# Second layer: value products of three of twelve key tiles as three rounded passes, scores three key tiles ahead, four buffers of probabilities

## The chip, the cores and the metric

The kernel runs on one core of one Trainium2 chip. A core has a matrix engine (PE, with its weight loads listed apart as PEld), a vector engine (DVE), a scalar engine (ACT), a general engine (POOL) and a queue engine for transfers (SP). They run side by side and order themselves by counting semaphores. The metric is the device time of one execution in microseconds (us), median of the runs. Lower is better.

## The reference, cut to what matters

Two layers of cross-attention and feed-forward over 16 batches of 56 tokens of width 256; the keys and values of both attentions come from the same context of 1500 rows of width 128 per batch. The change touches the attention of the second layer only:

```python
q = rmsnorm((hidden_states @ Wq).reshape(B, Sq, H, D), gq)      # 16 batches, 56 tokens, 16 heads, 128
k = rmsnorm((encoder_hidden_states @ Wk).reshape(B, Skv, H, D), gk)   # 1500 keys
v = (encoder_hidden_states @ Wv).reshape(B, Skv, H, D)
scores = jnp.einsum('bqhd,bkhd->bhqk', q, k) * scale
attn = jax.nn.softmax(scores, axis=-1)
out = jnp.einsum('bhqk,bkhd->bqhd', attn, v)
```

## The kernel before, in words

The kernel does not form k and v. The queries of a batch are folded through Wk beforehand, so that a score is a product of the folded query (128 x 896: 16 heads by 56 tokens, held in two halves of 448 columns) with the raw context, times one factor per key and head (`m.rk`). In the same way the probabilities multiply the raw context (`nat`, rows of keys), and Wv and Wo are applied once, after the loop.

`second_attention` goes through 16 batches, each of 12 key tiles of 125 keys. For one key tile:

- PE, `scores_half` (L1058 to L1060): each half of the scores is three passes of rounded 32-bit operands (type fp32r): query high by context low, query low by context high, high by high. "High" is the rounded value and "low" the rest, both made beforehand: `high_parts` on ACT (L906, L907), `low_parts` on POOL (L961), `query_low` on DVE (L998). The result lies in one of two pairs of PSUM banks (`slots`, t % 2).
- DVE, `scale_scores` (L993): multiplies by `m.rk` into one of two `scaled` buffers.
- ACT, `exp` (L918): writes the probabilities into one of NP = 3 buffers `P`.
- POOL, `add` (L968 for the first two tiles together, then L971): sums the probabilities into `acc`.
- PE, `values_half` (L1074): one full fp32 product per half, which shows as two records of PE, summed over the 12 tiles in `psO`.

Scores run LAG = 2 tiles ahead of the values: at step t, PE makes the scores of tile t+2 (from step 10 on those of the next batch), then the values of tile t. Scores of tile t+2 wait until tile t is scaled. At step 0 of a batch, PE also makes `sums` of the batch before (L1086: ones by `acc`), between scores and values.

The order of DVE is written out in its `body`. In step t it scales tile t+LAG. At step 0 it then takes the reciprocal of the sums of the batch before (`invert`, two instructions, L1006); at step 1, after the scaling, it multiplies the result of the batch before by it (`normalise`, two instructions, L1014, all operands in SBUF); at step 6 it runs `query_low` (at step 7 in batch 0). ACT copies the values out of PSUM at the end of a batch (`values_out`, L924) and makes the high parts for the batch after next at step NT - LAG. POOL makes the low part of the next context after the last add of a batch, then waits for `sums` before its first add (L968). Each engine takes its instructions in the order of the program.

Ahead of the loop, PE makes eight products of weights (`fold`), five before and three after the first scores; ACT and DVE copy them out (`keep_fold`).

Of the kernel before, what the change touches and what calls it, by code (L numbers as in the profile page):

```python
# [8 lines left out]
F32 = mybir.dt.float32  # L9
F32R = mybir.dt.float32r  # L10
BF16 = mybir.dt.bfloat16
U8 = mybir.dt.uint8
ALU = mybir.AluOpType
ACT = mybir.ActivationFunctionType
# [3 lines left out]
S, C = 1500, 128  # L18
H, HD, G0 = 16, 128, 8
KT, NT = 125, 12  # L20
QW, HALF = H * QS, H * QS // 2
# [70 lines left out]
def need(eng, sem, value):  # L92

    if isinstance(value, int) and value <= 0:
        return
    eng.wait_ge(sem, value)
# [27 lines left out]
def semaphores(sem, tag, names):  # L124

    return namedtuple("Semaphores", names)(*[sem(f"{tag}_{n}") for n in names])
# [290 lines left out]
def batches(eng, body):  # L417

    for b in range(B):
        body(b, b % 2, b + 1 < B, b + 2 < B)  # L420
# [9 lines left out]
def first_attention(nc, m, a, tag, sem):  # L430
# [6 lines left out]
    with ExitStack() as ctx:  # L437
# [8 lines left out]
        qlo = [m.qlo0, sb("qlo1", [C, QW], F32R)]  # L446
        P = [sb(f"probs{i}", [KT, QW], F32) for i in range(NP)]
        acc = sb("acc", [KT, QW], F32)
# [404 lines left out]
def second_attention(nc, m, a, tag, sem):  # L853

    s = semaphores(sem, tag, [
        "ld_land", "ld_nat0", "ld_nat1", "ctx_hi", "ctx_lo", "q_hi", "q_lo", "scores", "scaled", "probs", "pv", "acc",
        "den", "inv", "o_raw", "o_done", "fold_pe", "fold_act", "fold_dve", "y_pe", "y_act"])
    LAG, NP = 2, 3
    with ExitStack() as ctx:
        sb = lambda n, sh, dt: ctx.enter_context(nc.sbuf_tensor(f"{tag}_{n}", sh, dt))  # L860
        psum = lambda n, sh: ctx.enter_context(nc.psum_tensor(f"{tag}_{n}", sh, F32))
# [3 lines left out]
        nat = [m.nat0, sb("nat1", [KT, NT, C], F32)]  # L865
        qhi = [sb(f"qhi{i}", [C, QW], F32R) for i in range(2)]
        qlo = [sb(f"qlo{i}", [C, QW], F32R) for i in range(2)]
        scaled = [sb(f"scaled{i}", [KT, QW], F32) for i in range(2)]
        P = [sb(f"probs{i}", [KT, QW], F32) for i in range(NP)]
        acc = sb("acc", [KT, QW], F32)  # L870
        inv = sb("inv", [C, 2, HALF], F32)
        norm_banks = psum("norm", [128, 2, 512])
        slots = psum("slots", [128, 2, 2, 512])
        psO = psum("psO", [128, 2, 512])
# [25 lines left out]
        @block.scalar  # L900
        def _(act):
            def high_parts(b, par):

                need(act, s.ld_land, 16 * b)
                need(act, s.scores, NT * (b - 1))
                act.activation(chi[par][:, :], land[:, :], ACT.Copy).then_inc(s.ctx_hi, 1)  # L906
                act.activation(qhi[par][:, :], m.qs[:, bass.ds(b, 1), :, :].rearrange("p o h q -> p (o h q)"),  # L907
                               ACT.Copy).then_inc(s.q_hi, 1)

            def exp(b, par, t):  # L910

                need(act, s.pv, NT * b + t + 1 - NP)
                if t >= NP:
                    need(act, s.acc, (NT - 1) * b + max(1, t - NP))
                else:
                    need(act, s.acc, (NT - 1) * b + t + 1 - NP)
                act.wait_ge(s.scaled, NT * b + t + 1)
                act.activation(P[t % NP][:, :], scaled[t % 2][:, :], ACT.Exp).then_inc(s.probs, 1)  # L918

            def values_out(b):  # L920

                act.wait_ge(s.pv, NT * b + NT)
                dst = m.qs[:, bass.ds(b, 1), :, :].rearrange("p o (a h) q -> p (o a) (h q)", a=2)
                act.activation(dst, psO[:, :, 0:HALF], ACT.Copy).then_inc(s.o_raw, 1)  # L924

            def body(b, par, nxt, nxt2):
                for t in range(NT):
                    if b == 0 and t == 3:
                        high_parts(1, 1)
                    if t == NT - LAG and nxt2:  # L930
                        high_parts(b + 2, par)
                    for bt, tt in tile_ahead(LAG, b, t):
                        exp(bt, bt % 2, tt)
                values_out(b)

            def keep_fold(i):

                act.wait_ge(s.fold_pe, i + 1)
                act.activation(fold_rows(i), fold_bank(i), ACT.Copy).then_inc(s.fold_act, 1)

            first = S // 4
            act.activation(chi[0][:, 0:first], land[:, 0:first], ACT.Copy).then_inc(s.ctx_hi, 1)
            act.activation(qhi[0][:, :], m.qs[:, 0, :, :].rearrange("p h q -> p (h q)"), ACT.Copy).then_inc(s.q_hi, 1)
            act.activation(chi[0][:, first:S], land[:, first:S], ACT.Copy).then_inc(s.ctx_hi, 1)
            for i in (0, 2, 4):
                keep_fold(i)
            exp(0, 0, 0)
            keep_fold(6)
            exp(0, 0, 1)
            batches(act, body)  # L950
            act.wait_ge(s.ctx_lo, B + 1)
            for i in range(KC):
                act.wait_ge(s.y_pe, i + 1)
                act.activation(land[:, HALF * i:HALF * i + HALF], slots[:, 0, i, 0:HALF], ACT.Copy).then_inc(s.y_act, 1)
# [30 lines left out]
        @block.vector  # L985
        def _(dve):
            def scale_scores(b, par, t):

                dve.wait_ge(s.scores, NT * b + t + 1)
                need(dve, s.probs, NT * b + t - 1)  # L990
                src = slots[0:KT, t % 2, :, 0:HALF].rearrange("p a (h q) -> p a h q", q=QS)
                rk = m.rk[:, bass.ds(b, 1), t, :].rearrange("p o (a h) -> p (o a) h", a=2).unsqueeze(3)
                dve.tensor_tensor(scaled[t % 2][:, :].rearrange("p (a h q) -> p a h q", a=2, q=QS), src,  # L993
                                  rk.to_broadcast([KT, 2, H // 2, QS]), ALU.mult).then_inc(s.scaled, 1)

            def query_low(b, par):
                dve.wait_ge(s.q_hi, b + 1)
                dve.tensor_tensor(qlo[par][:, :], m.qs[:, bass.ds(b, 1), :, :].rearrange("p o h q -> p (o h q)"),  # L998
                                  qhi[par][:, :].bitcast(F32), ALU.subtract).then_inc(s.q_lo, 1)

            def invert(b):

                dve.wait_ge(s.den, b + 1)
                need(dve, s.o_done, 2 * b)
                for half in range(2):
                    dve.reciprocal(inv[:, half, :], norm_banks[:, half, 0:HALF]).then_inc(s.inv, 1)  # L1006

            def normalise(b):

                dve.wait_ge(s.o_raw, b + 1)  # L1010
                o = m.qs[:, bass.ds(b, 1), :, :].rearrange("p o (a h) q -> p (o a) (h q)", a=2)
                for half in range(2):
                    dve.wait_ge(s.inv, 2 * b + half + 1)
                    dve.tensor_tensor(o[:, half, :], inv[:, half, :], o[:, half, :], ALU.mult).then_inc(s.o_done, 1)  # L1014

            def body(b, par, nxt, nxt2):
                start = isinstance(b, int) and b == 0
                for t in range(NT):
                    for bt, tt in tile_ahead(LAG, b, t):
                        scale_scores(bt, bt % 2, tt)  # L1020
                    if t == 0 and not start:
                        invert(b - 1)
                    if t == 1 and not start:
                        normalise(b - 1)
                    if nxt and t == (7 if b == 0 else 6):
                        query_low(b + 1, 1 - par)

            def keep_fold(i):

                dve.wait_ge(s.fold_pe, i + 1)  # L1030
                dve.tensor_copy(fold_rows(i), fold_bank(i)).then_inc(s.fold_dve, 1)

            query_low(0, 0)
            for i in (1, 3):
                keep_fold(i)
            for t in range(LAG):
                scale_scores(0, 0, t)
            for i in (5, 7):
                keep_fold(i)
            batches(dve, body)  # L1040
            invert(B - 1)
            normalise(B - 1)

        @block.tensor
        def _(pe):
# [18 lines left out]
            def values_half(b, par, t, half):  # L1064
                if half == 0:
                    pe.wait_ge(s.probs, NT * b + t + 1)
                    if t == 0:
                        need(pe, (s.ld_nat0, s.ld_nat1)[par], 8 * (b + par))
                        need(pe, s.o_raw, b)
                        if b == 0:  # L1070
                            pe.wait_ge(s.fold_act, 2)
                            pe.wait_ge(s.fold_dve, 2)
                cols = slice(HALF * half, HALF * half + HALF)
                last = pe.matmul(psO[:, half, 0:HALF], nat[par][:, t, :], P[t % NP][:, cols], start=t == 0, stop=t == NT - 1)  # L1074
                if half == 1:
                    last.then_inc(s.pv, 1)

# [885 lines left out]
```

## Time and profile before

| What | Value |
|---|---|
| Median of 3 runs | 2141.82 us (2140.28 to 2142.17) |
| The profiled execution | 2140.49 us |
| Its span | 2138.7 us |
| PE busy in the span | 2089.7 us (98%) |
| DVE busy | 1638.7 us (77%) |
| ACT busy | 1082.3 us (51%) |
| POOL busy | 1417.7 us (66%) |

The loop of the second attention lies between about 1370 and 1930 us of the span. A row of a timeline gives start, duration, engine, line, operation, output and inputs with their shapes, how many instructions were merged into it (x4), and in brackets how long the engine had been idle before it and who released it. Matmul records overlap, since an end includes the way through the array; the distance between starts tells what a pass costs. Rows of a line give minimum, median and maximum duration in ns.

### The profile page before, as it was taken

How to read it: one execution, taken by the hardware profiler on the slowest of the kernel's cores; microseconds unless marked ns; L12 is line 12 of the kernel's file. 1: busy time of each engine (PE TensorE's matmuls, PEld its weight loads, DVE VectorE, ACT ScalarE, POOL GpSimd, SP SyncE). 2: the span in 40 equal slices, each digit the busy share in tenths (PEclk: the TensorE clock that was granted, in tenths of full speed). 3: DMA queues.
4: the chain of work that ended last, by engine and by line, in shares of the span. 5: the costliest groups of instructions: out<-in, count | busy, mean ns of one | idle time of the engine just before them, and what ended most of it. 6: DMA issues, size and time to landing. Idle time of an engine off the chain costs nothing. (4 is left out here: it accounts for less than half of the span.)

```text
span 2138.7 us, 27497 instructions
## 1 busy us (share of the span) xinstructions
PE 2089.7 (98%) x8514; PEld 1520.4 (71%) x8514; DVE 1638.7 (77%) x2584; ACT 1082.3 (51%) x3401; POOL 1417.7 (66%) x1062
## 2 busy tenths in 40 slices
PE   7999999999999999999999899999999999999999
PEld 7777677777777777777777468666666666665998
DVE  4889999999999999999997765556666665642577
ACT  3565555655665556555556328543434444332433
POOL 1477787778777878788777336287877878761221
PEclk9999999999999999999999999999999999999999
DMA  3000000000000000000001310011111111101110
GB/s 134 30 15 16 29 29 15 24 21 30 16 29 15 30 29 15 15 29 30 15 11 40 135 54 1 30 44 57 45 43 55 33 58 29 44 0 52 38 53 25
DMA packets 15140, 75.64 MB, mean 35 GB/s; under 512 B 1746, under 2 KB 2114, under 8 KB 13986
## 3 DMA queue, kind: packets, MB, share of 16 engines
q1 hardware_dynamic: 14994, 73.89, 10.5%
q8 instruction: 68, 1.11, 0.2%
q14 instruction: 78, 0.64, 0.1%
HBM read 72.97 MB, written 0.92 MB: 35 GB/s over the span
## 5 line engine op out<-in xcount | busy, mean ns | idle before, releaser
L539 ACT ACTIVATE l_prod_act<-l_prod_act 125x128 f32<-125x128 f32 x1152 | 343.8, 301 | 353.0 <-DVE l_prod_act L714 353.0
L634 POOL TENSOR_TENSOR l_prod<-l_prod 125x256 f32<-125x256 f32 x480 | 350.4, 737 | 239.6 <-DVE l_prod L714 239.4
L971 POOL TENSOR_TENSOR l_acc<-l_acc,l_probs 125x896 f32<-125x896 f32 x160 | 346.3, 2164 | 81.4 <-ACT l_probs L918 65.9
L714 DVE TENSOR_TENSOR l_prod<-l_side,xq 125x512 f32<-125x512 f32 x480 | 325.6, 678 | 45.1 <-PE l_side L823 38.7
L993 DVE TENSOR_TENSOR l_scaled<-l_slots,rk 125x896 f32<-125x896 f32 x192 | 207.0, 1084 | 198.8 <-PE l_slots L1060 198.7
L918 ACT ACTIVATE l_probs<-l_scaled 125x896 f32<-125x896 f32 x192 | 183.1, 954 | 318.7 <-DVE l_scaled L993 293.5
L628 POOL TENSOR_TENSOR l_acc<-l_acc,l_probs 125x896 f32<-125x896 f32 x160 | 339.2, 2120 | 0.0
L557 ACT ACTIVATE l_probs<-l_slots,mask_bias 125x448 f32<-125x448 f32 x384 | 225.5, 624 | 59.7 <-PE l_slots L775 54.1
L684 DVE SCALAR_TENSOR_TENSOR top<-l_side,mask_bias,top 125x448 f32<-125x448 f32 x330 | 217.1, 666 | 8.0 <-PE l_side L806 8.0
L539 ACT ACTIVATION_READ_ACCUMULATOR l_prod_act<-l_prod_act 125x1 f32 x1152 | 219.1, 190 | 0.0
L723 DVE TENSOR_REDUCE l_msq<-l_prod 125x4 f32<-125x256 f32 x480 | 197.3, 412 | 22.3 <-POOL l_prod L634 22.3
L714 DVE TENSOR_TENSOR l_prod_act<-l_side,xq 125x512 f32<-125x512 f32 x288 | 197.3, 685 | 16.6 <-PE l_side L823 13.9
L1058 PE MATMUL l_slots<-l_qhi,l_clo 128*125 128x448 f32 x384 | 203.2, 529 | 0.0
L822 PE MATMUL l_side<-norm_lo,l_chi 128*125 128x512 f32 x384 | 198.3, 516 | 0.4 <-DVE l_prod L714 0.2
L822 PE MATMUL l_side<-norm_lo,chi 128*125 128x512 f32 x384 | 196.4, 511 | 0.2
L784 PE MATMUL l_psO<-l_probs,spare 125*128 125x448 f32 x384 | 174.6, 539 | 0.0
L784 PE MATMUL l_psO<-l_probs,l_nat 125*128 125x448 f32 x384 | 174.6, 539 | 0.0
L1074 PE MATMUL l_psO<-l_probs,nat 125*128 125x448 f32 x384 | 160.0, 538 | 0.0
L1074 PE MATMUL l_psO<-l_probs,l_nat 125*128 125x448 f32 x384 | 159.7, 538 | 0.0
L823 PE MATMUL l_side<-norm_hi,chi 128*125 128x512 f32 x384 | 151.5, 394 | 0.0
L823 PE MATMUL l_side<-norm_hi,l_chi 128*125 128x512 f32 x384 | 151.3, 394 | 0.0
L1059 PE MATMUL l_slots<-l_qlo,l_chi 128*125 128x448 f32 x384 | 140.4, 366 | 0.0
(261 smaller groups left out, 4619.4 us busy)
## 6 DMA issues: line engine op xcount, KB each, us to landing
land<-in_ctxT SPq DMA_DIRECT2D x32, 750.0 KB, 4.2
l_nat<-in_ctxN SPq DMA_DIRECT2D x16, 750.0 KB
post_we<-in_experts SPq DMA_DIRECT2D x20, 384.0 KB, 3.0
spare<-in_ctxN SPq DMA_DIRECT2D x8, 750.0 KB
nat<-in_ctxN SPq DMA_DIRECT2D x8, 750.0 KB
spare<-in_wo SPq DMA_DIRECT2D x2, 2048.0 KB, 9.0
spare<-in_wqT SPq DMA_DIRECT2D x4, 512.0 KB, 8.8
mid_fac<-in_factors SPq DMA_DIRECT2D x1, 2048.0 KB, 7.6
```

What stands on the lines that cost most here:

```text
L539: last = act.activation(whole, whole, ACT.Copy, accum_out=msq[:, t, 4 * g + c:4 * g + c + 1])
L557: act.activation(P[t % NP][:, HALF * i:HALF * i + HALF], bank_of("S", t, i)[0:KT, 0:HALF], ACT.Exp, bias=m.mask_bias[:, b, t:t + 1]).then_ ...
L628: pool.tensor_tensor(acc[:, :], acc[:, :], P[t % NP][:, :], ALU.add).then_inc(s.acc, 1)
L634: pool.tensor_tensor(buf[:, :, 0:C // 2], buf[:, :, 0:C // 2], buf[:, :, C // 2:C], ALU.add).then_inc(s.half_sum, 1)
L684: dve.scalar_tensor_tensor(top[:, cols], bank, bias, top[:, cols], ALU.add, ALU.max).then_inc(s.side_dve, 1)
L714: dve.tensor_tensor(to[:, :, :], bank, xt.unsqueeze(1).to_broadcast([KT, 4, C]), ALU.mult).then_inc(s.side_dve, 1)
L784: last = pe.matmul(psO[:, half, 0:HALF], nat[b % 2][:, t, :], P[t % NP][:, cols], start=t == 0, stop=t == NT - 1)
L822: pe.matmul(bank[0:KT, :], chi[b % 2][:, keys], m.norm_lo[:, cols], start=True, stop=False)
L823: last = pe.matmul(bank[0:KT, :], chi[b % 2][:, keys], m.norm_hi[:, cols], start=False, stop=True)
L971: pool.tensor_tensor(acc[:, :], acc[:, :], P[t % NP][:, :], ALU.add).then_inc(s.acc, 1)
L993: dve.tensor_tensor(scaled[t % 2][:, :].rearrange("p (a h q) -> p a h q", a=2, q=QS), src, rk.to_broadcast([KT, 2, H // 2, QS]), ALU.mult) ...
L1074: last = pe.matmul(psO[:, half, 0:HALF], nat[par][:, t, :], P[t % NP][:, cols], start=t == 0, stop=t == NT - 1)
```

## The change

LAG becomes 3 and NP becomes 4. For key tiles 3, 6 and 9 of each batch the fp32 product of a half is replaced by three rounded passes: values low by probabilities high, values high by probabilities low, high by high. The parts of the probabilities are made per tile, high on ACT after the exponential, low on DVE; those of the values once per batch for the three tiles together (125 x 384), for the next batch at step 11.

```diff
-    LAG, NP = 2, 3
+    LAG, NP = 3, 4
+    SPLIT = [3, 6, 9]
+    tiles_split = slice(3, 10, 3)
...
+            def probs_high(b, t):
+                at = SPLIT.index(t)
+                act.wait_ge(s.probs, NT * b + t + 1)
+                act.activation(phi[at % 2][:, :], P[t % NP][:, :], ACT.Copy).then_inc(s.p_hi, 1)
+            def values_high(b):
+                need(act, (s.ld_nat0, s.ld_nat1)[b % 2], 8 * (b + b % 2))
+                need(act, s.pv, NT * (b - 1) + SPLIT[-1] + 1 if b > 0 else 0)
+                act.activation(nat_hi[:, :, :], nat[b % 2][:, tiles_split, :], ACT.Copy).then_inc(s.p_hi, 1)
...
                     for bt, tt in tile_ahead(LAG, b, t):          # ACT
                         exp(bt, bt % 2, tt)
+                        if tt in SPLIT:
+                            probs_high(bt, tt)
+                    if t == SPLIT[-1] + 2 and nxt:
+                        values_high(b + 1)
                 values_out(b)
...
+            values_high(0)
             for i in (0, 2, 4):
                 keep_fold(i)
             exp(0, 0, 0)
             keep_fold(6)
             exp(0, 0, 1)
+            exp(0, 0, 2)
...
+            def probs_low(b, t):
+                at = SPLIT.index(t)
+                dve.wait_ge(s.p_hi, (len(SPLIT) + 1) * b + at + 2)
+                dve.tensor_tensor(plo[at % 2][:, :], P[t % NP][:, :], phi[at % 2][:, :].bitcast(F32), ALU.subtract).then_inc(s.p_lo, 1)
+            def values_low(b):
+                dve.wait_ge(s.p_hi, (len(SPLIT) + 1) * b + 1)
+                dve.tensor_tensor(nat_lo[:, :, :], nat[b % 2][:, tiles_split, :], nat_hi[:, :, :].bitcast(F32),
+                                  ALU.subtract).then_inc(s.p_lo, 1)
...
                     for bt, tt in tile_ahead(LAG, b, t):          # DVE
                         scale_scores(bt, bt % 2, tt)
+                    if t + 2 in SPLIT:
+                        probs_low(b, t + 2)
+                    if t == SPLIT[-1] + 2 and nxt:
+                        values_low(b + 1)
                     if t == 0 and not start:
                         invert(b - 1)
                     if t == 1 and not start:
                         normalise(b - 1)
...
             query_low(0, 0)
+            values_low(0)
...
                 cols = slice(HALF * half, HALF * half + HALF)     # PE
-                last = pe.matmul(psO[:, half, 0:HALF], nat[par][:, t, :], P[t % NP][:, cols], start=t == 0, stop=t == NT - 1)
+                if t in SPLIT:
+                    at = SPLIT.index(t)
+                    pe.wait_ge(s.p_lo, (len(SPLIT) + 1) * b + at + 2)
+                    pe.matmul(psO[:, half, 0:HALF], nat_lo[:, at, :], phi[at % 2][:, cols], start=False, stop=False)
+                    pe.matmul(psO[:, half, 0:HALF], nat_hi[:, at, :], plo[at % 2][:, cols], start=False, stop=False)
+                    last = pe.matmul(psO[:, half, 0:HALF], nat_hi[:, at, :], phi[at % 2][:, cols], start=False, stop=False)
+                else:
+                    last = pe.matmul(psO[:, half, 0:HALF], nat[par][:, t, :], P[t % NP][:, cols], start=t == 0, stop=t == NT - 1)
```

## Rows read from the trace of the kernel before

**Rows 1.** Busy time by engine in 1720 to 1800 us: busy (count), granted clock.
```profile
core 0: us, PE busy (x) PEld busy (x) DVE busy (x) ACT busy (x) POOL busy (x), PEclk, DMA share, GB/s
1720.00:1800.00 80.00, 80.00 (x291) 53.77 (x290) 53.77 (x42) 31.87 (x34) 61.88 (x28) 1.00 0.19 56
```

**Rows 2.** Timeline of PE, one key tile of the second attention.
```profile
1630.23 1.67 PE L1074 MATMUL l_psO<-l_probs,l_nat 125*128 125x448 f32 x4
1631.94 0.36 PE L1059 MATMUL l_slots<-l_qlo,l_chi 128*125 128x448 f32 x1
1632.14 0.36 PE L1060 MATMUL l_slots<-l_qhi,l_chi 128*125 128x448 f32 x1
1632.94 1.67 PE L1074 MATMUL l_psO<-l_probs,l_nat 125*128 125x448 f32 x4
```

**Rows 3.** Timeline of PE, rounded passes with 128 weight columns, last stage.
```profile
2060.16 0.36 PE L1808 MATMUL post_bk<-post_xhi,post_wlo 128*128 128x448 f32 x1
2060.36 0.36 PE L1809 MATMUL post_bk<-post_xlo,post_whi 128*128 128x448 f32 x1
```

**Rows 4.** Timeline of all engines, start of a batch (its values from 1616.48).
```profile
1614.98 1.67 PE L1086 MATMUL l_norm<-l_acc,ones 125*128 125x448 f32 x4
1616.48 1.67 PE L1074 MATMUL l_psO<-l_probs,l_nat 125*128 125x448 f32 x4
1616.68 5.77 DVE L1006 RECIPROCAL l_inv<-l_norm 128x448 f32<-128x448 f32 x2 [0.41 <-PE l_norm L1086]
1616.79 2.10 POOL L968 TENSOR_TENSOR l_acc<-l_probs 125x896 f32<-125x896 f32 x1 [2.09 <-PE l_norm L1086]
1619.04 2.09 POOL L971 TENSOR_TENSOR l_acc<-l_acc,l_probs 125x896 f32<-125x896 f32 x1
1622.37 1.03 DVE L993 TENSOR_TENSOR l_scaled<-l_slots,rk 125x896 f32<-125x896 f32 x1
1623.31 1.15 DVE L1014 TENSOR_TENSOR qs<-l_inv,qs 128x448 f32<-128x448 f32 x2
1623.51 0.95 ACT L918 ACTIVATE l_probs<-l_scaled 125x896 f32<-125x896 f32 x1 [6.17 <-DVE l_scaled L993]
1623.76 0.36 PE L1059 MATMUL l_slots<-l_qlo,l_chi 128*125 128x448 f32 x1
1624.54 14.02 POOL L971 TENSOR_TENSOR l_acc<-l_acc,l_probs 125x896 f32<-125x896 f32 x6 [3.42 <-ACT l_probs L918]
```

**Rows 5.** Instructions by line: ns minimum/median/maximum.
```profile
L998 DVE TENSOR_TENSOR l_qlo<-qs,l_qhi x16: 1144/2425/2452, 1366.5 to 1874.6; 128x896 fp32r<-128x896 f32 x16
L1014 DVE TENSOR_TENSOR qs<-l_inv,qs x32: 560/612/621, 1417.2 to 1931.3; 128x448 f32<-128x448 f32 x32
```

**Rows 6.** Timeline of DVE and POOL around one `query_low`.
```profile
1599.16 5.04 POOL L971 TENSOR_TENSOR l_acc<-l_acc,l_probs 125x896 f32<-125x896 f32 x2
1599.80 2.42 DVE L998 TENSOR_TENSOR l_qlo<-qs,l_qhi 128x896 fp32r<-128x896 f32 x1
```

**Rows 7.** Timeline of DVE and POOL between the layers; last row: L1186 by line.
```profile
1289.54 1.56 DVE L1186 TENSOR_SCALAR mid_xn<-x,mid_meanvar,mid_rstd 112x256 f32<-112x256 f32 x2
1289.73 1.21 POOL L1264 TENSOR_TENSOR mid_sql<-mid_sq,mid_sqh 128x448 fp32r<-128x448 f32 x1 [0.26 <-ACT mid_sqh L1335]
1289.86 1.24 DVE L1186 TENSOR_SCALAR mid_xn<-x,mid_meanvar,mid_rstd 112x256 f32<-112x256 f32 x1
...
L1186 DVE TENSOR_SCALAR mid_xn<-x,mid_meanvar,mid_rstd x16: 400/410/1246, 1245.4 to 1289.9; 112x256 f32<-112x256 f32 x16
```

**Rows 8.** Groups of instructions by line and shape: count, busy us, mean ns.
```profile
L907 ACT ACTIVATE l_qhi<-qs 128x896 fp32r<-128x896 f32 x15 | 14.0, 936 | 0.0
L523 ACT ACTIVATE l_chi<-land 128x375 fp32r<-128x375 f32 x8 | 4.0, 502 | 0.0
L961 POOL TENSOR_TENSOR l_clo<-land,l_chi 128x1500 fp32r<-128x1500 f32 x15 | 51.1, 3409 | 0.0
```

**Rows 9.** The longest waits of PE for a vector result, and the windows around it.
```profile
PE pre_bk L405 <- DVE top L276: 3.4, 1, 3.4
PE mid_bk L1441 <- POOL mid_sql L1264: 2.2, 3, 1.1
...
21.00:24.00 3.00, 2.27 (x12) 0.50 0.32 133
24.00:27.00 3.00, 3.00 (x18) 0.57 0.16 66
```

More of the change, by code:

```diff
@@ L855, in second_attention @@
     s = semaphores(sem, tag, [
-        "ld_land", "ld_nat0", "ld_nat1", "ctx_hi", "ctx_lo", "q_hi", "q_lo", "scores", "scaled", "probs", "pv", "acc",
+        "ld_land", "ld_nat0", "ld_nat1", "ctx_hi", "ctx_lo", "q_hi", "q_lo", "scores", "scaled", "probs", "p_hi", "p_lo", "pv", "acc",
         "den", "inv", "o_raw", "o_done", "fold_pe", "fold_act", "fold_dve", "y_pe", "y_act"])
-    LAG, NP = 2, 3
+    LAG, NP = 3, 4
+    SPLIT = [3, 6, 9]
+    tiles_split = slice(3, 10, 3)
     with ExitStack() as ctx:
@@ L869, in second_attention @@
         P = [sb(f"probs{i}", [KT, QW], F32) for i in range(NP)]
+        phi = [sb(f"phi{i}", [KT, QW], F32R) for i in range(2)]
+        plo = [sb(f"plo{i}", [KT, QW], F32R) for i in range(2)]
+        nat_hi = sb("nat_hi", [KT, len(SPLIT), C], F32R)
+        nat_lo = sb("nat_lo", [KT, len(SPLIT), C], F32R)
         acc = sb("acc", [KT, QW], F32)
```

## The prediction

> **What bounds the kernel now.** I read the busy shares by engine first, then those of the loop that is changed, then its timeline tile by tile. In the loop PE is busy all the time at the full granted clock, while DVE has 67% and POOL 77% [rows 1]: what counts is PE's own work, and any moment at which another engine is late for it. In a tile [rows 2] the four fp32 records begin at 1630.23 and the sixth score pass ends where the next four begin, 1632.94: 2.71 us. The sums, also four fp32 records, take from 1614.98 to 1616.48, 1.50 us [rows 4]; the six score passes have the rest, 0.20 us each (1631.94 to 1632.14). So PE needs 12 x 2.73 + 1.50 = 34.3 us for a batch and idles hardly at all. The one place with little slack is the start of a batch. There two reciprocals hold DVE for 5.77 us, the scaling behind them ends at 1623.40 (1622.37 + 1.03), and the score passes that wait for it are about 0.1 us late: from the value product's start at 1621.94 the second score pass is normally 1.71 us off [as in rows 2] and here begins at 1623.76, 1.82 us off [rows 4].
>
> **Part 1, PE work.** A half of a split tile drops two fp32 records (0.75 us) for three rounded passes. Weights 128 columns wide do not slow such a pass: 0.20 us [rows 3]. With 0.205 a tile goes from 1.50 to 1.23 us, 0.27 less; 3 tiles x 16 batches x 0.27 = 13.0 us off PE. The number of score tiles stays the same.
>
> **Part 2, added side work of a batch.** ACT: three copies of 125x896 at 0.94 and one of 125x384 at about 0.51 us [rows 8], 3.3 us on an engine with 40% in the loop [rows 1]; hidden. DVE: three subtractions of the form of `query_low`, both inputs in SBUF, 1.14 us alone and 2.42 us usually [rows 5], and one of 384 columns, about 0.5 us. That puts DVE at some 30 of 36 us, so its order matters.
>
> **Part 3, what DVE's two-input work costs beside POOL.** `query_low` begins at 1599.80, in the middle of an add that began at 1599.16 and takes 2.10; it ends at 1602.22, that is 0.96 us after that add ended at 1601.26; and the second add, due by then, ends at 1604.20, 1.98 us after the subtraction [rows 6]. They don't share: one waits until the other is through. The Trainium skill says the same (SBUF — State Buffer, "Who interferes with whom"): a DVE instruction with two inputs in SBUF contends with a GpSimd instruction that reads SBUF, and the lock is held for the whole instruction by whichever came first. By that rule, and the trace agrees here, an instruction of DVE pays for the whole add in flight.
>
> **Part 4, the start of a batch.** Zero is the start of the first value product (1616.48 in [rows 4]); handing over costs 0.20 us from PE to DVE, 0.11 from DVE to ACT, 0.08 from ACT to POOL, about 0.16 from DVE to PE, and DVE begins the next instruction some 0.09 before the end of one (all from [rows 4], the last two from 1622.37 + 1.03 = 1623.40 against 1623.76 - 0.20 and 1623.31).
> - DVE: with LAG 3, scaling of tile 3 comes before the reciprocals and is off their way; they still begin at 0.20; the scaling of tile 4 takes 5.89 to 6.92, the place that tile 3 had.
> - PE: values 0 to 1.50, scores 4 to 2.73, values 1 to 4.23, scores 5 to 5.47, values 2 to 6.97; scores 6 wait for scaled tile 4 until 7.08, as late as today, and end at 8.31.
> - POOL: adds begin at 0.31, 2.56 and 4.80 (2.10 each); the third ends at 6.90. The fourth waits for exp of tile 4 (7.03 to 7.98) and is due at 8.06.
> - DVE: low part of tile 3 from 6.83, POOL quiet from 6.90: 1.14 us, ends at 8.0. Values 3 on PE are due at 8.31 and end at 9.54: in time.
> - Then `normalise`, before the scaling of tile 5. Today it meets no add: POOL is idle until 1624.54 [rows 4], and the 32 instructions take 560 to 621 ns [rows 5]. Now the first half runs from 7.91 to 8.52, and the fourth add comes in at 8.06 and stands first in line when the half is done. It ends at 8.52 + 1.98 = 10.50, and only then comes the second half: 10.50 + 0.48 = 10.98. Scaling of tile 5 ends near 11.95, and scores 7, which need it, start at 12.1 instead of 9.54.
>
> That is a stall of 2.55 us in each of the 15 batches that have one before them: 38 us. Bounds for this wait, of which the trace has no case: below, both halves pass before the add, 0.6 us (9.04 for `normalise`, 10.0 for the scaling, 10.15 for PE); above, both halves wait for an add each, 2 x 2.1 more than alone, but the fifth add itself needs tile 5, so the second add can't be there, which leaves about 2.8. I take 2.55, since in [rows 7] an instruction of POOL that comes in during the third of four DVE instructions (1289.73, between 1289.54 and 1289.94) gets ahead of the fourth, which takes 1.24 instead of 0.41 us.
>
> What follows in the batch has slack. Behind the stall, the low part of tile 6 waits at most one add (about 2.3 us) and is done at 16.4 while values 6 are due at 18.9; `query_low`, scaling of tile 10 and the low part of tile 9 end at 24.9 for values 9 at 26.8. At the end POOL's low part of the context (3.41 us [rows 8]) ends at about 35.0; `values_low` is due at 34.9, ends at 35.45, and scaling of tile 3 at 36.4, when the reciprocals begin anyway (36.3 + 0.2). Each 0.1 us by which POOL is later there costs 15 x 0.1. A batch thus takes 34.3 + 0.1 - 0.8 + 2.55 = 36.2 us.
>
> **Part 5, outside the steady loop.** Before the first batch, the third score tile waits for the first to be scaled, and the last `fold` for a copy that DVE makes after scaling tile 2: I reckon the first values about 2.0 us later, of which 1.23 is a score tile made ahead: 0.8 us lost. Batch 0 has no `normalise`.
>
> **Sum.** -13.0 + 38.3 + 0.8 = +26 us. On the profiled execution (2140.5) that is 2166.6; the median of the runs is 1.3 above it: 2168.
>
> **Rivals.**
> - *Both halves before the add* (the other side). If DVE keeps its port between two instructions that overlap by 0.09 us, `normalise` is through at 9.04. The stall is then 0.6 us: -13.0 + 15 x 0.6 + 0.8 = -3.2, 2139. It decides at a stall of 0.8 us (12.2/15). For it: the second half is issued at 8.43, before the first has ended. Against: [rows 7]. 17%.
> - *Sharing.* If both engines just slow down, `normalise` runs 2.1 times as long behind 8.06 (2.42 against 1.14 in [rows 5]) and ends at 10.2, 0.8 earlier than forecast: stall 1.8, +15, 2157. [Rows 6] speak against it. With it go cases in which only part of the batches meet the add. 14%.
> - *POOL late at the end.* If its low part of the context slips by 0.5 us, `values_low` and all behind it slip too: another 7 us, 2175. Part of the forecast's own range. 6%.
> - *The clock falls.* After PE had waited 3.4 us for DVE near the start, the granted clock went to 0.50, the 1.2 GHz level, for the windows from 21 us on; after waits of 1.1 us at most it did not [rows 9]. 2.55 us lies between. Some 6 us at half the clock would cost 3 us a batch: +45 more, 2213. 5%.
> - *The split saves nothing*, because weights of 125 rows or fp32r operands written by ACT and DVE make the passes dearer: it would need 0.25 us a pass, seen nowhere. 2%.
>
> **How the numbers follow.** The forecast itself has 56%, with 2162 to 2176 as its own range (stall of 2.3 to 2.8, POOL's slip). Adding sharing and the first rival takes the range from 2137 to 2177, which leaves out the clock and tails. A change under 0.2%, 4.3 us, can't be told from none in such a measurement. The first rival is 3 us faster, so it counts mostly as no change (0.11) and partly as faster (0.08); the rest, 0.81, is slower.
>
> **What would show it.** The value rows of tiles 3, 6, 9 as six passes 0.20 us apart. Pairs of `normalise` of some 3.1 us from start to end in place of 1.15, with an add between. PE idle before the scores of tile 7, released by the scaling, 2.5 us x 15; values never waiting for a low part. A batch from reciprocal to reciprocal of 36.2 us against 34.3. I am wrong if `normalise` stays at 1.2 us, if the stall is at another tile, or if the clock leaves 1.00 in the loop.

## The result, and the profile after

The changed kernel takes 2186.1 us (median of 4 runs, 2185.2 to 2187.0) against 2142.0 before: ratio 1.0207, 95% interval 1.0189 to 1.0225. It is 44 us slower; forecast were 26 us, 2168, with a range that ended at 2177.

The loop was to be read first, and within it one batch against another. The first fence has the windows of two neighbouring batches of the changed kernel, from the start of the values of one to that of the next, and below them that of an earlier batch.

```profile
core 0: us, PE busy (x) PEld busy (x) DVE busy (x) ACT busy (x) POOL busy (x), PEclk, DMA share, GB/s
1638.59:1672.73 34.14, 33.80 (x132) 24.18 (x130) 25.04 (x22) 17.48 (x19) 28.96 (x12) 1.00 0.14 42
1672.73:1710.37 37.64, 35.38 (x132) 25.33 (x131) 29.25 (x22) 17.57 (x19) 28.73 (x12) 0.95 0.15 45
1413.73:1449.97 36.24, 33.96 (x132) 24.18 (x130) 27.22 (x22) 17.47 (x19) 28.71 (x12) 1.00 0.15 44
```

All do the same work. The second takes 3.5 us longer, PE is idle for 2.3 us of it, and the granted clock averages 0.95 in place of 1.00. Of the 15 batches that have one before them, 13 are like it. One more, from 1413.73, has the wait but keeps the clock. Only the one from 1638.59 has neither. The timeline of the second, with the rows that answer to [rows 4]:

```profile
1672.73 1.67 PE L1122 MATMUL l_psO<-l_probs,nat 125*128 125x448 f32 x4
1672.93 5.77 DVE L1042 RECIPROCAL l_inv<-l_norm 128x448 f32<-128x448 f32 x2
1678.62 1.03 DVE L1017 TENSOR_TENSOR l_scaled<-l_slots,rk 125x896 f32<-125x896 f32 x1
1679.56 1.08 DVE L1029 TENSOR_TENSOR l_plo<-l_probs,l_phi 125x896 fp32r<-125x896 f32 x1
1680.56 3.07 DVE L1050 TENSOR_TENSOR qs<-l_inv,qs 128x448 f32<-128x448 f32 x2
1680.79 2.35 POOL L995 TENSOR_TENSOR l_acc<-l_acc,l_probs 125x896 f32<-125x896 f32 x1 [1.19 <-ACT l_probs L924]
1681.04 0.37 PE L1118 MATMUL l_psO<-l_phi,l_nat_lo 125*128 125x448 f32 x1
1682.05 0.37 PE L1120 MATMUL l_psO<-l_phi,l_nat_hi 125*128 125x448 f32 x1
1683.55 2.08 DVE L1017 TENSOR_TENSOR l_scaled<-l_slots,rk 125x896 f32<-125x896 f32 x2
1684.68 0.73 PE L1099 MATMUL l_slots<-l_qhi,l_clo 128*125 128x448 f32 x1 [2.27 <-DVE l_scaled L1017]
1685.22 0.57 PE L1100 MATMUL l_slots<-l_qlo,l_chi 128*125 128x448 f32 x1
1685.59 0.57 PE L1101 MATMUL l_slots<-l_qhi,l_chi 128*125 128x448 f32 x1
```

The pair of multiplications takes 3.07 us where it took 1.15 [rows 4], with an add between its halves: its second half, seen by itself, runs from 1681.10 to 1683.63, and the add ends at 1683.14. Behind it the scaling of tile 5 begins at 1683.55, and PE, through with the values of tile 3 at 1682.25, starts the scores of tile 7 only at 1684.68. From then on the passes are 0.37 us apart instead of 0.20: the clock has fallen. The window over that stretch, columns as above but PE alone:

```profile
1684.70:1688.10 3.40, 3.40 (x8) 0.51 0.00 0
```

In the batch from 1638.59 the exponential of tile 4 came 0.28 us later, for a reason that the trace doesn't show, and with it the add. Its record now begins as good as together with that of the second multiplication (1646.93 and 1646.95), where it was 0.3 us ahead of it in the other batch (1680.79 and 1681.10):

```profile
1645.42 1.08 DVE L1029 TENSOR_TENSOR l_plo<-l_probs,l_phi 125x896 fp32r<-125x896 f32 x1
1646.42 1.16 DVE L1050 TENSOR_TENSOR qs<-l_inv,qs 128x448 f32<-128x448 f32 x2
1646.93 2.61 POOL L995 TENSOR_TENSOR l_acc<-l_acc,l_probs 125x896 f32<-125x896 f32 x1 [1.46 <-ACT l_probs L924]
1646.95 0.62 DVE L1050 TENSOR_TENSOR qs<-l_inv,qs 128x448 f32<-128x448 f32 x1
1648.62 0.47 PE L1099 MATMUL l_slots<-l_qhi,l_clo 128*125 128x448 f32 x1 [0.34 <-DVE l_scaled L1017]
```

(The last DVE row is the second half alone, which the row before the add counts too.) Here the pair took 1.16 us, the add had to wait instead (2.61 us), PE was 0.5 us late and the clock stayed up.

### The profile page after: what moved, and what is told of

The parts are those of the page before. It is cut to its first block and busy times, and to the rows that moved or that the text cites. A ratio compares the mean times of both kernels' runs of the same rounds, so it can differ in the third digit from the quotient of the medians.

```text
span 2185.2 us, 27879 instructions
## 1 busy us (share of the span) xinstructions
PE 2103.0 (96%) x8610; PEld 1553.4 (71%) x8610; DVE 1751.1 (80%) x2648; ACT 1130.8 (52%) x3465; POOL 1443.1 (66%) x1062
## 5 line engine op out<-in xcount | busy, mean ns | idle before, releaser
L995 POOL TENSOR_TENSOR l_acc<-l_acc,l_probs 125x896 f32<-125x896 f32 x160 | 371.8, 2324 | 76.1 <-ACT l_probs L924 63.4
L628 POOL TENSOR_TENSOR l_acc<-l_acc,l_probs 125x896 f32<-125x896 f32 x160 | 339.1, 2120 | 0.0
L1099 PE MATMUL l_slots<-l_qhi,l_clo 128*125 128x448 f32 x384 | 193.0, 503 | 34.2 <-DVE l_scaled L1017 32.7
L784 PE MATMUL l_psO<-l_probs,l_nat 125*128 125x448 f32 x384 | 174.6, 539 | 0.0
L1101 PE MATMUL l_slots<-l_qhi,l_chi 128*125 128x448 f32 x384 | 145.7, 380 | 0.0
L1100 PE MATMUL l_slots<-l_qlo,l_chi 128*125 128x448 f32 x384 | 145.5, 379 | 0.0
L1099 PEld LDWEIGHTS l_slots<-l_qhi,l_clo 128*125 128x125 f32 x384 | 74.0, 193 | 77.8 <-DVE l_scaled L1017 49.0
```

Source lines behind the costliest of these rows:

```text
L628: pool.tensor_tensor(acc[:, :], acc[:, :], P[t % NP][:, :], ALU.add).then_inc(s.acc, 1)
L784: last = pe.matmul(psO[:, half, 0:HALF], nat[b % 2][:, t, :], P[t % NP][:, cols], start=t == 0, stop=t == NT - 1)
L995: pool.tensor_tensor(acc[:, :], acc[:, :], P[t % NP][:, :], ALU.add).then_inc(s.acc, 1)
L1099: pe.matmul(out, clo[par][:, keys], qhi[par][:, cols], start=True, stop=False)
```

## The experiments

The theory after the result had two links: (1) an add of POOL gets in between the two multiplications of DVE and holds the second back, because both have two inputs in SBUF; (2) the wait of PE that this makes is just long enough to bring the clock down, which costs 1.5 us more. The rivals: the longer lead, or the load on DVE as such, or dear split passes; and for the clock, that it only shows the idle time.

**The lead and the buffers alone** (`SPLIT = []`, the parts of the values left out).

> The score lead of three tiles and the four buffers alone, no split tile. Theory (port order, then clock): the two multiplications follow the scaling of tile 4 at once, from 6.83 to 7.95 after the start of a batch's values, before the add that is due at 8.06; no collision, the clock stays at 1.00. Only the start-up cost of about 1 us is left: 2143 us, within 0.2% of before. Rival (the longer lead itself is the cost, by the order of DVE or by more buffers in flight): 10 us or more above before, with PE stalled once per batch.

2142.8 us, ratio 1.0007 (0.9997 to 1.0016). The pair and the add, from its timeline:

```profile
1660.28 1.15 DVE L1045 TENSOR_TENSOR qs<-l_inv,qs 128x448 f32<-128x448 f32 x2
1661.51 4.34 POOL L990 TENSOR_TENSOR l_acc<-l_acc,l_probs 125x896 f32<-125x896 f32 x2 [1.19 <-ACT l_probs L922]
```

The pair is through 0.08 us before the add. The lead costs about 1 us by itself, which can't be told from nothing.

**The inverse kept in PSUM.** The sums, which overwrite it there, now wait for the multiplications.

```diff
-                    dve.reciprocal(inv[:, half, :], norm_banks[:, half, 0:HALF]).then_inc(s.inv, 1)
+                    dve.reciprocal(norm_banks[:, half, 0:HALF], norm_banks[:, half, 0:HALF]).then_inc(s.inv, 1)
...
-                    dve.tensor_tensor(o[:, half, :], inv[:, half, :], o[:, half, :], ALU.mult).then_inc(s.o_done, 1)
+                    dve.tensor_tensor(o[:, half, :], norm_banks[:, half, 0:HALF], o[:, half, :], ALU.mult).then_inc(s.o_done, 1)
...
-                need(pe, s.inv, 2 * b)
+                need(pe, s.o_done, 2 * b)
```

> The changed kernel, but the reciprocals are written back into PSUM, so that each of the two multiplications has only one input in SBUF; order and amount of work are the same. Theory: they take 0.6 to 0.7 us each beside the adds, 1.2 to 1.4 us a pair instead of 3.07; the wait before the scores of tile 7 falls from 2.45 to 0.6 to 0.9 us, and the clock stays at 1.00: -13.3 + 15 x 0.75 + 2.5 = about 0, 2142 us (2138 to 2146). Rival (DVE is simply overloaded by the low parts, or the split passes are dear): stays above 2170.

2141.5 us, ratio 0.9999 (0.9990 to 1.0009): 44 us are back by the place of one operand.

```profile
1661.10 1.15 DVE L1049 TENSOR_TENSOR qs<-l_norm,qs 128x448 f32<-128x448 f32 x2
1661.34 2.11 POOL L994 TENSOR_TENSOR l_acc<-l_acc,l_probs 125x896 f32<-125x896 f32 x1 [1.23 <-ACT l_probs L923]
1663.30 0.47 PE L1098 MATMUL l_slots<-l_qhi,l_clo 128*125 128x448 f32 x1 [0.34 <-DVE l_scaled L1016]
```

The add begins 0.24 us behind the pair and runs beside it; neither is longer for it. The order, the low parts and the split passes are those of the changed kernel, so none of these costs the 44 us by itself.

**One multiplication instead of two**, the inverse in SBUF as in the changed kernel (counts of `o_done` halved).

```diff
-                for half in range(2):
-                    dve.wait_ge(s.inv, 2 * b + half + 1)
-                    dve.tensor_tensor(o[:, half, :], inv[:, half, :], o[:, half, :], ALU.mult).then_inc(s.o_done, 1)
+                dve.wait_ge(s.inv, 2 * b + 2)
+                dve.tensor_tensor(o, inv[:, :, :], o, ALU.mult).then_inc(s.o_done, 1)
```

> The changed kernel with the two multiplications of 448 columns written as one of 896, at the same place, all inputs in SBUF. Theory (an add gets in only between two instructions of DVE, never inside one): it starts at 7.83, before the add that is due at 8.06, takes 1.1 us, and the add waits instead; the wait before the scores of tile 7 is 0.5 to 0.6 us, the clock stays at 1.00: 2142 us (2139 to 2144), as with the reciprocals in PSUM. Rival (two-input work beside adds is slow by sharing): the pair still takes 2.4 us or more, 2160 or above.

2142.3 us, ratio 1.0003 (0.9994 to 1.0012).

```profile
1661.32 1.08 DVE L1049 TENSOR_TENSOR qs<-l_inv,qs 128x896 f32<-128x896 f32 x1
1661.56 2.82 POOL L995 TENSOR_TENSOR l_acc<-l_acc,l_probs 125x896 f32<-125x896 f32 x1 [1.19 <-ACT l_probs L924]
```

The same operands, the same place, the same collision: whole, the multiplication isn't touched, and the add pays (2.82 against 2.10 us in [rows 4]). That rules out sharing, under which both would be slow, and shows the gap between two instructions as the place of the loss.

**PE kept busy while it waits** (8, then 4 passes, whose results nothing uses).

```diff
                 for t in range(NT):
+                    if t == 4 and not start:
+                        pe.wait_ge(s.inv, 2 * b)
+                        for i in range(8):
+                            pe.matmul(norm_banks[0:KT, i % 2, 0:HALF], chi[par][:, 0:KT], qhi[par][:, 0:HALF], start=True, stop=True)
```

> The changed kernel with eight more rounded passes (1.64 us) on PE, put between the values of tile 3 and the scores of tile 7, where PE waits; their result is used nowhere. They shorten the idle time from 2.45 to about 0.8 us and leave the wait's end where it is. Theory (the fall of the clock is a cost of its own, 1.5 us in 13 batches): clock 1.00 all through, 2186 - 20 = 2166 us, although more is computed. Rival (the granted clock only echoes the idle time, the whole loss is the wait): 2186 us or more.

2169.3 us, ratio 1.0130 (1.0115 to 1.0145): 17 us less than the changed kernel, with 120 matmuls more.

> As filler8, with four unused passes (0.82 us) in place of eight: PE is idle for 1.6 us before the scores of tile 7. Which idle time brings the clock down is open between 1.1 us (it held, in the kernel before) and 2.27 us (it fell). If 1.6 us is short enough the clock stays at 1.00 and the time is that of filler8, 2169 us; if not, 2186 us as for the changed kernel.

2169.5 us, ratio 1.0131 (1.0117 to 1.0145). With four passes PE is idle for 1.46 us; its timeline, then the window around it:

```profile
1674.33 0.97 PE L1144 MATMUL l_norm<-l_qhi,l_chi 128*125 128x448 f32 x4
1676.77 0.47 PE L1099 MATMUL l_slots<-l_qhi,l_clo 128*125 128x448 f32 x1 [1.46 <-DVE l_scaled L1017]
```

```profile
1674.00:1678.00 4.00, 2.54 (x13) 1.00 0.00 0
```

So the clock is a cost of its own, beside the wait that stays.

**The two multiplications one step later**, in both forms (`if t == 2 and not start: normalise(b - 1)`). With the inverse in SBUF:

> The changed kernel with the two multiplications one step later, behind the scaling of tile 5, and both inputs still in SBUF: the position alone, without the change of place of the reciprocals. Theory (the port goes to whoever asked first, for a whole instruction): the first multiplication is due at 8.9 while the fourth add runs till 10.16, the fifth add is due before it ends and gets in ahead of the second; the pair ends at 13.1, scaling of tile 6 at 14.1, and PE waits 1.9 us before the scores of tile 8 in place of tile 7: 2132 + 15 x 1.9 = 2160 us if the clock holds, up to 2180 if it falls. Rival (only the place at step 1 is bad, one step of slack is enough): 2132 us as with the reciprocals in PSUM.

2169.0 us, ratio 1.0130 (1.0116 to 1.0144).

```profile
1676.28 4.28 DVE L1050 TENSOR_TENSOR qs<-l_inv,qs 128x448 f32<-128x448 f32 x2
1680.48 2.08 DVE L1017 TENSOR_TENSOR l_scaled<-l_slots,rk 125x896 f32<-125x896 f32 x2
1681.61 0.47 PE L1099 MATMUL l_slots<-l_qhi,l_clo 128*125 128x448 f32 x1 [1.73 <-DVE l_scaled L1017]
```

The pair now meets two adds, 4.28 us, and PE waits a tile later: its scores start 14.16 us after the values; the scaling before them was expected to end at 14.1. The time is 9 us above the 2160 that I gave for it; a batch takes 35.9 in place of 35.5 us, and I haven't followed the rest. With the inverse in PSUM:

> As the one with the reciprocals in PSUM, and the two multiplications come one step later, behind the scaling of tile 5. Theory: scaling of tile 5 ends at about 9.0 and that of tile 6 at 11.2, before PE needs them at 9.5 and 12.3: no wait in the batch is left, the gain of the split shows: 2142 - 13.3 + 2.5 = 2131 us (2129 to 2134). Rival (the split saves less than 0.27 us a tile in place): 2138 or more.

2131.9 us, ratio 0.9957 (0.9942 to 0.9972): faster than both kernels, by 10 and by 54 us. One of its batches:

```profile
1649.56:1683.16 33.60, 33.60 (x131) 24.27 (x130) 26.03 (x22) 17.48 (x19) 28.53 (x12) 1.00 0.17 50
```

Its batches are 33.6 us apart against 34.34 before, and PE is busy all through. Of the 0.81 us that three split tiles save, 0.74 is there.

**One multiplication, one step later.**

> The single multiplication, one step later, behind the scaling of tile 5. Theory: it asks at 8.86 while the fourth add runs to 10.2, goes next, ends at 11.1; scaling of tile 6 ends at 12.1, as PE comes to need it at 12.3: no wait or one of 0.1 us, 2132 to 2134 us. In two instructions the same place gave 2169. Rival: an add gets in ahead of it as well, 2145 or more.

2138.9 us, ratio 0.9982 (0.9973 to 0.9992): between theory and rival. The multiplication waits for the one add in flight, and only that:

```profile
1659.73 5.03 POOL L995 TENSOR_TENSOR l_acc<-l_acc,l_probs 125x896 f32<-125x896 f32 x2 [1.19 <-ACT l_probs L924]
1660.50 2.30 DVE L1049 TENSOR_TENSOR qs<-l_inv,qs 128x896 f32<-128x896 f32 x1
```

It ends at 1662.80, and batches are 33.9 us apart, 0.3 more than with the inverse in PSUM (15 x 0.3 = 4.5 us). I had reckoned that the scaling behind it would be just in time; it is just late. The rest comes from elsewhere. The ten runs fall into two groups, four of 2135.3 to 2136.4 us and six of 2138.8 to 2139.9, and the profiled one is of the second. In its trace the clock falls in the last stage, in the middle of dense work of PE (PE alone):

```profile
1984.00:1990.00 6.00, 6.00 (x57) 0.99 0.00 0
1990.00:1996.00 6.00, 6.00 (x19) 0.50 0.00 0
```

It is low for 6.8 us there, which costs about 3.4 us (an estimate, half of it). That is the distance between the groups, and their mean granted clocks, 0.996 to 0.997 and 0.994 to 0.995, go with it. The trace of the run before this one has 3.4 us of it at the same place, that of the mended start below none.

**The split with the old lead** (`LAG, NP = 2, 3`).

> The changed kernel with the score lead and the buffers of before (2 and 3), so the split alone. Theory: the low part of a tile must follow its own scaling at once, so DVE stands still for the exponential and the copy of ACT, 2.1 us per split tile, with the scaling of the next tile queued behind it; with the adds in between PE waits some 7 us a batch: 2230 us or more. Rival (the longer lead is not needed): 2190 or less.

2242.7 us, ratio 1.0473 (1.0454 to 1.0492). DVE, from its waits:

```profile
DVE l_plo L1028 <- ACT l_phi L930: 94.8, 45, 3.0
PE l_psO L1117 <- DVE l_plo L1028: 44.7, 28, 2.8
```

DVE stands 2.1 us before each low part, with the next scaling queued behind it. A batch takes 41.0 us, and the clock falls here too (0.92 on average over the one from 1493.50), so part of the 101 us is the clock's. The longer lead is what makes this split worth having.

**The start mended.** `values_high(0)` after `exp(0, 0, 2)`, `values_low(0)` after the last `keep_fold`, `query_low` at step 8 in batch 0.

> psum_step2 with the start mended: the parts of the values of batch 0 are made after the first scalings and copies rather than before them, and the low part of the next queries comes at step 8 rather than 7 in batch 0. Theory: of the 2.5 us lost before and in batch 0 it gives back up to 2 us: 2130 us. Rival (the start is bound by the third score tile and the copies of the folded weights anyway): 2132, no change.

2132.1 us, ratio 0.9954 (0.9941 to 0.9968): no difference from 2131.9. From the first high part of the stage to the first reciprocal it takes 48.1 us against 48.7, and this stage begins 0.6 us later in the profiled run (1366.58 against 1366.01), so that the gain is not to be seen.

**Four split tiles.**

> best3 with four split tiles (3, 5, 7, 9) in place of three. Theory: 16 x 0.27 = 4.4 us less on PE, if DVE, with some 32 of 33.3 us a batch, is never late: 2128 us. Rival (DVE becomes the bound, since each low part waits for an add in flight): 2135 or more, with PE released by the scaling several times a batch.

2147.1 us, ratio 1.0026 (1.0016 to 1.0037): the rival. Its low parts by line, then the waits of PE in the loop:

```profile
L1028 DVE TENSOR_TENSOR l_plo<-l_probs,l_phi 125x896 fp32r<-125x896 f32 x64 | 124.1, 1939 | 21.3 <-ACT l_phi L929 20.9
```

```profile
PEld l_slots L1098 <- DVE l_scaled L1016: 10.5, 15, 0.7
PE l_psO L1117 <- DVE l_plo L1028: 8.2, 16, 1.1
```

A low part takes 1.94 us on average, most of the excess over 1.08 spent behind an add; PE now waits for low parts in every batch (34.2 us against 33.6), 9 us in all. The start, measured as for the run before, takes 52.9 us against 48.1, with PE idle for 3.8 us in batch 0. In this order of DVE three tiles are what it can feed; a fourth at another place was not tried.

## Why the prediction was wrong

The direction and the path were right; the size was not, because a rival came on top of the forecast and the start cost more.

- **Split passes.** Six passes from 1681.04 to 1682.25, 0.20 us each. Forecast: -13.0 us. Holds.
- **Start of a batch.** In us from the start of the values (1672.73): multiplications at 7.83 (7.91 forecast), the add at 8.06 (8.06), the pair's end at 10.90 (10.98), scaling of tile 5 to 11.9 (11.95), scores of tile 7 at 11.95 (12.1). The stall was 2.43 us where 2.55 were forecast, in 14 of 15 batches: 34.0 in place of 38.3 us, and 0.5 in the one left. Which of the bounds would hold was the open point, and the rows on which I decided it [rows 7] decided it rightly; the rule of the Trainium skill that I cited beside [rows 6] (SBUF — State Buffer, "Who interferes with whom"), that the lock is held for a whole instruction, is borne out by the single multiplication, which no add breaks into.
- **The rival on the other side** happened once in 15 batches, at 34.14 us a batch as worked out for it (34.2), and for a shift of 0.28 us.
- **The step that failed: the clock.** The sum put it at nothing. I had it as a rival with 5%, on the ground that 2.55 us lay between a wait of 1.1 us, after which the clock held, and one of 3.4 us, after which it fell [rows 9]. That misread the second. The wait of 3.4 us runs from 18.34 to 21.73, and finer windows of the trace of before (PE alone) show the clock falling within the first 1.7 us of it (PE had worked there with gaps, 1.3 of the 3 us up to 19.00):

```profile
19.00:20.00 1.00, 0.00 (x0) 0.89 0.80 331
20.00:21.00 1.00, 0.00 (x0) 0.50 0.33 135
```

  So the trace didn't speak for a clock that holds through 2.55 us. In the changed kernel it fell in 13 of the 14 stalled batches, which was also one of the signs of being wrong that the prediction named. I also gave it too long a duration: 6 us and 3 us a batch, where it lasted about 3.4 us. From the scores of tile 7 to those of tile 8 it takes 4.05 us (1684.68 to 1688.73) against 2.48 in the batch from 1638.59 that kept its clock: 1.57 us a batch, 20.4 us in all. Each of the two fillers takes back 17 of these.
- **The start** was set at 0.8 us. It is 2.4: the first values come 2.2 us later within the stage, of which 1.23 are a tile made ahead, since a low part of 384 columns met POOL and took 2.63 us ahead of the copies; and in batch 0 the low part of tile 9 and `query_low` in one step make PE wait 1.4 us, which I had passed over with "batch 0 has no `normalise`".
- The reckoning then: -13.0 + 34.0 + 0.5 + 20.4 + 2.4 = 44.3 us, measured 44.1. The first two batches above check it apart: 37.64 - 34.14 = 3.50, and (2.43 - 0.51) + 1.57 = 3.49.

## What to carry to other kernels

Before moving work on DVE that reads two operands in SBUF, look where POOL's instructions fall beside it: each such instruction can wait for one in flight, so one long instruction is worth more than two short ones, and an operand left in PSUM avoids the meeting altogether. Where a change makes the matrix engine wait again and again for more than 2 us, price the fall of the clock with the wait, not as an unlikely extra; and look in narrow windows when in a wait the clock fell, since a wide one hides it. And a change that loses may hold a gain behind one wait: here a PSUM operand and one step of delay turned +44 us into -10.

## What was not expected of the hardware

- The clock fell after PE had been idle for 2.24 to 2.41 us (by the record) amid otherwise dense work, to the 1.2 GHz level for 3.4 us, in 13 batches, and held in one after 2.25 us. It held after 1.46 us (four fillers) and 1.73 us (the pair one step later, clock 1.00 in the window around it), there once after 2.00 us too.
- Idle time isn't all that decides: in the last stage the clock fell with PE busy all the time and its longest wait, of 1.19 us, 7 us back, and in other runs of the same stage it didn't. What brings it down stays open here.
- An add that POOL asks for while DVE is in the first of two instructions gets in before the second, although the record of that one begins 0.09 us before the first ends: 3.07 us in place of 1.15. When the two records began 0.02 us apart, DVE went first.
- An instruction of DVE that was held back ends about its pure streaming time after the add: here 10.90 against 10.41 for the add's end, 0.49 us for 448 columns.
